# Two attention and expert layers on one core: setup taken apart into calls among the first batches, loads reordered, the order of calls written out

## The reference

```
x = x + xattn(_layernorm(x), ctx, bias (4,16,512,77), mask, L0 weights)      # softmax over 77
x = x + ffn(_layernorm(x), w_router, wi, wo)     # top 2 of 8 experts, capacity 64, gelu, 128->512->128
x = x + xattn(_layernorm(x), ctx, attn_mask (512,77) with padding, L1 weights)
x = x + ffn(_layernorm(x), gate_w, gate_b, expert_w, expert_b)   # top 2 of 8 true + 2 null experts
```

## Time and profile before

| | |
|---|---|
| median of three runs | 414.07 us |
| the profiled execution | 414.41 us, span 412.6 us |
| TensorE matmul busy | 335.0 us (81%), 3625 instructions |
| VectorE busy | 267.6 us (65%) |
| GpSimd busy | 188.9 us (46%) |
| ScalarE busy | 172.1 us (42%) |
| HBM read | 17.53 MB |

### The profile page before, as it was taken

One profiled execution on the slowest core, in us unless ns is written; L12 is line 12 of the kernel. 1 busy time (PEld: TensorE's weight loads), 2 busy tenths in 40 slices (PEclk: granted clock), 3 DMA queues, 4 the chain that ended last, 5 costly groups with the idle time before them and its releaser, 6 DMA issues.

```text
span 412.6 us, 8817 instructions
## 1 busy us (share of the span) xinstructions
PE 335.0 (81%) x3625; PEld 250.1 (61%) x3633; DVE 267.6 (65%) x629; ACT 172.1 (42%) x317; POOL 188.9 (46%) x211
## 2 busy tenths in 40 slices
PE   3985597587899999999999989999776886787382
PEld 2982366265679777788778867886634553454120
DVE  0132558849666855766766766775898889877632
ACT  3000323132736546374646636563623443353222
POOL 9202534364737334646536443520763376254214
PEclk9999996959999999999999999999995999699867
DMA  3996314130504022000000000000000000000000
GB/s 98 251 366 207 93 39 132 32 101 0 132 2 132 4 54 79 0 3 2 0 3 1 3 2 2 2 2 0 4 1 25 2 2 1 27 2 0 27 1 25
DMA packets 26363, 19.15 MB, mean 46 GB/s; under 512 B 1909, under 2 KB 24275, under 8 KB 26323
## 3 DMA queue, kind: packets, MB, share of 16 engines
q1 hardware_dynamic: 26163, 18.56, 15.4%
q0 software_dynamic: 160, 0.02, 0.3%
HBM read 17.53 MB, written 1.05 MB: 45 GB/s over the span
## 4 chain that ended last, share of the span: by engine, by line
PE 60%; DVE 21%; ACT 9%; issue 4%; POOL 3%; SPq 1%; DMA 1%; POOLq 0%; DVEq 0%; ACTq 0%
PE PB L809 10%; PE HBK L891 8%; PE EBK L906 7%; DVE SC L1228 7%; PE SP L790 6%; ACT PT L533 5%; PE SP L771 4%; PE HBK L914 4%; DVE mx L1230 3%; DVE rc L1236 3%; PE HBK L956 2%; PE SP L775 2%; PE MB L748 2%; PE EBK L956 2%; PE PB L815 1%
## 5 line engine op out<-in xcount | busy, mean ns | idle before, releaser
L351 POOL TENSOR_TENSOR SC<-SC,mx 128x1232 f32<-128x1232 f32 x32 | 72.0, 2250 | 136.9 <-DVE mx L1230 136.8
L533 ACT COPY PT<-SP 128x512 f32<-128x512 f32 (+1 forms) x96 | 44.4, 521 | 41.0 <-PE SP L790 41.0
L790 PE MATMUL SP<-ident,SC 128*128 128x128 f32 x320 | 48.1, 298 | 12.3 <-ACT SC L525 6.4
L790 PEld LDWEIGHTS SP<-ident,SC 128*128 128x128 f32 x320 | 40.4, 154 | 21.8 <-issue 12.5
L525 ACT ACTIVATE SC<-SC 128x1232 f32<-128x1232 f32 x32 | 39.3, 1229 | 33.5 <-POOL SC L351 33.4
L1230 DVE TENSOR_REDUCE mx<-SC 128x16 f32<-128x1232 f32 x32 | 46.0, 1436 | 1.1
L1236 DVE RECIPROCAL rc<-PB 128x128 f32<-128x128 f32 x32 | 30.5, 952 | 16.5 <-PE PB L809 16.5
L809 PE MATMUL PB<-PT,VB 128*32 128x128 f32 x768 | 30.8, 299 | 12.5 <-ACT PT L533 11.7
L891 PE MATMUL HBK<-ein,wi_s 128*128 128x128 f32 x256 | 36.8, 287 | 2.6 <-ACT hT L551 2.6
L891 PEld LDWEIGHTS HBK<-ein,wi_s 128*128 128x128 f32 x256 | 31.0, 191 | 10.9 <-ACT hT L551 5.5
L551 ACT ACTIVATE hT<-HBK 128x512 f32<-128x512 f32 x32 | 19.1, 597 | 41.1 <-PE HBK L891 41.0
(11 more groups left out here) (174 smaller groups left out, 577.1 us busy)
## 6 DMA issues: line engine op xcount, KB each, us to landing
BI<-in_fside_Bx16xSxS SPq DMA_DIRECT2D x8, 1232.0 KB, 6.3
wi_s<-in_L_ffn_wi SPq DMA_DIRECT2D x1, 2048.0 KB, 10.8
X<-in_x SPq DMA_DIRECT2D x4, 256.0 KB, 3.6
out<-acc SPq DMA_DIRECT2D x4, 256.0 KB, 2.1
MI<-in_mask_BxSxS_ik SPq DMA_DIRECT2D x8, 77.0 KB, 7.0
ew_s<-in_L_ffn_expert_w SPq DMA_DIRECT2D x1, 512.0 KB, 4.9
ctxn<-in_ctx SPq DMA_DIRECT2D x1, 154.0 KB
am<-in_fside_SxS SPq DMA_DIRECT2D x1, 154.0 KB, 2.5
```

The costliest lines, as they stand in the source:

```text
L351: g.tensor_tensor(S4, S4, m4, ALU.subtract).then_inc(s["shifted"], 1)
L533: sc.copy(PT[:, c0:c1, :].rearrange("p c t -> p (c t)"), SP[:, n, 0:(c1 - c0) * P]).then_inc(s["PTs"], 1)
L790: last = te.transpose(SP[:, n, (c - c0) * P:(c - c0 + 1) * P], SC[i % 2][:, c * P:(c + 1) * P], ident[:])
```

## The change

The setup's steps become functions that are called among the calls of the first two batches, most constants are filled by VectorE instead of GpSimd (`fill`), the loads have semaphores by group and a new order, and `stretch` is gone: each engine's program is a list of calls (309 on TensorE, 197 on VectorE, 219 on ScalarE, 119 on GpSimd, from 296, 188, 212 and 112). The arithmetic is the same. Values of batch 0 go to PB and EBK, of the others to HBK and EBK; keys of layer 1 to EBK. Some calls have further waits (`gelu` on `m_eo`, `f_xTcopy` on `m_logits`, `a_xTr` on the routing), since the order no longer implies them. The gate bias and expert bias loads move from GpSimd's queue to SP's.

```diff
@@ sync
-            for n in range(4):
-                sp.dma_start(W[:, n, :], w0[n]).then_inc(s["ld_w"], 16)
...
-            load_bias(0)
...
+            load_x(0, "ld_x0")
             sp.dma_start(ctxn[:], ctx_in.rearrange("b j d -> j b d")).then_inc(s["ld_ctx"], 16)
+            load_w(0, 1, "ld_wa")
+            load_w(0, 0, "ld_wa")
+            load_col(0, 1, "ld_ca")
+            load_col(0, 0, "ld_ca")
+            load_mask(0, 0)
+            load_bias(0, 0)
...
+            load_mask(0, 1)
+            load_bias(0, 1)
...
+            load_mask(1, 0)
+            load_bias(1, 0)
+            load_mask(1, 1)
+            load_bias(1, 1)
+            sp.dma_start(wo_s[:], wo.rearrange("e (c f) d -> f e c d", c=FC)).then_inc(s["ld_moe"], 16)
...
@@ scalar
+                if f > 0 or e >= 4:
+                    act.wait_ge(s["m_eo"], NE // 2 * f + (e - 4) // 2 + 1)
...
@@ tensor
-            stretch(0, 0, None, None, None, None)
-            stretch(1, 0, 0, 0, None, None)
-            for a in range(2, B):
-                stretch(a, 0, a - 1, 0, a - 2, 0)
...
+            turn_ctx()
+            turn_weights((0, 1), "ld_wa", 0)
+            a_xTr(0)
+            keys(0)
+            query(0, 0)
+            attn_scores(0, 0, 0)
+            turn_weights((2, 3, 6), "ld_wb", 1)
+            values(0)
+            attn_scores(0, 1, 0)
+            turn(0, 0, 0)
+            turn_weights((4, 5, 7), "ld_wc", 3)
+            turn(0, 0, 1)
+            value_bias(0)
+            attn_scores(0, 2, 0)
+            keys(1)
+            weigh_values(0, 0)
+            value_bias(1)
+            turn(0, 1, 0)
+            values(1)
...
@@ vector
+            def fill():
+                for t, x in ((half[:], -0.5), (identb[:], 0.0), (rowmask[:], 1.0), (incl[:], 1.0), (strict[:], 1.0),
...
+                    v.memset(t, x).then_inc(s["c_dset"], 1)
...
+            fill()
+            a_stats(0, 0)
+            a_norm(0, 0)
+            copy_first()
+            scale_q(0, 0)
+            softmax_max(0, 0, 0)
+            spread_bv()
+            softmax_max(0, 1, 0)
+            add_bias(0)
+            mask_values(0)
...
```

More of the change, by code:

```diff
@@ L489, in _ @@
[L489 to L492 removed]
+            identity()
+            identity_bf16()
+            head_rows()
+            a_rstd(0)
+            block_rows()
+            mask_out(0, 0)
+            block_keys(0, 0, "k_kb")
+            block_keys(1, 0, "k_kb")
+            shift(0, 0)
+            mask_out(0, 1)
+            shift(0, 1)
@@ L677, in _ @@
[L677 to L686 removed]
+            copy_ctx(0, 1)
@@ new lines, in _ @@
+            attn_scores(1, 1, 0)
+            project(0, 3, 0)
+            turn(1, 0, 0)
+            values(3)
+            f_xTr(0)
+            turn(1, 0, 1)
+            logits0(0)
+            attn_scores(1, 2, 0)
+            weigh_values(1, 0)
+            turn(1, 1, 0)
+            positions(0)
+            project(1, 0, 0)
+            turn(1, 1, 1)
+            attn_scores(1, 3, 0)
+            dispatch(0, 0)
+            weigh_values(1, 1)
+            turn(1, 2, 0)
+            turn(1, 2, 1)
@@ new lines, in _ @@
+            positions(2)
+            up(1, 7)
+            turn(3, 1, 0)
+            down(1, 3)
+            turn(3, 1, 1)
+            combine(1, 0)
+            project(3, 0, 0)
+            combine(1, 1)
+            weigh_values(3, 1)
+            attn_scores(3, 3, 0)
+            dispatch(2, 0)
+            a_xTr(4)
+            turn(3, 2, 0)
+            project(3, 1, 0)
+            turn_C(2, 0)
+            turn(3, 2, 1)
+            dispatch(2, 1)
+            weigh_values(3, 2)
+            turn_C(2, 1)
@@ new lines, in _ @@
+            turn_C(2, 2)
+            turn(3, 3, 0)
+            turn_C(2, 3)
+            turn(3, 3, 1)
+            project(3, 2, 0)
+            up(2, 0)
+            query(4, 1)
+            weigh_values(3, 3)
+            up(2, 1)
+            attn_scores(4, 0, 1)
+            up(2, 2)
+            project(3, 3, 0)
+            up(2, 3)
+            attn_scores(4, 1, 1)
+            up(2, 4)
+            down(2, 0)
+            up(2, 5)
+            f_xTr(3)
+            down(2, 1)
+            up(2, 6)
@@ new lines, in _ @@
+            logits0(3)
+            turn(4, 0, 0)
+            turn(4, 0, 1)
+            down(2, 2)
+            attn_scores(4, 2, 1)
+            weigh_values(4, 0)
+            positions(3)
+            up(2, 7)
+            turn(4, 1, 0)
+            turn(4, 1, 1)
+            down(2, 3)
+            attn_scores(4, 3, 1)
+            combine(2, 0)
+            project(4, 0, 1)
+            combine(2, 1)
+            weigh_values(4, 1)
+            dispatch(3, 0)
+            turn(4, 2, 0)
+            turn(4, 2, 1)
```

1582 lines of the change are left out of this document (953 added, 629 removed).

## The result

The changed kernel took **381.23 us** (median of four runs, 378.92 to 382.82) beside 413.99 for the kernel before (413.46 to 415.3): a ratio of 0.920, with a 95% interval of 0.915 to 0.925. The forecast was 383.8 with a range of 369 to 396. The profiled execution took 381.17 us with a span of 379.5. The same kernel went again with the experiments: 383.4 us (378.11 to 390.28, ratio 0.928, 0.921 to 0.935). Medians and ranges here count every execution, while a ratio compares only those within 1.5% of the fastest of their kernel, so a median and its ratio need not agree.

A forecast was written before the change was run, and what follows sets the result against it. It took setup alone to hold the first 30.8 us, the attention chain to pace the opening and TensorE the middle. Terms −25.8 + 1.2 − 3 − 1 − 2 = −30.6 from 414.4 gave 383.8 us, range 369 to 396.

The forecast's parts named there:

- Term A: Start of batch 0: with X loaded first, first scores at 13.0 us instead of 38.8, −25.8 us.
- The −24.4: Start of batch 0: the start's gain if batch 0's normalising waits for GpSimd's rowmask selects, 0.35 us each.
- Term B: First scores to first up-projection: setup matmuls moved in are nearly free, +76.3 us instead of +75.1, so +1.2 us.
- I keep the low level until about 30: Opening: assumes TensorE's clock stays at its low level, 1.2 GHz, until about 30 us.
- The first L720 at the low level: Opening: a sign the forecast is right, the first of the setup's value matmuls running at the low clock level.
- Term C: Middle, 113.9 to 300 us: the new call order takes 3 of 10.6 us idle, −3, between 0 and −8.
- Terms D and E: 300 to 380 us, VectorE's list almost unchanged: −1; the end, last tile's scores and expert matmuls reordered: −2.
- middle stretches under 45: Middle: a sign that the order gains more than counted, batches under 45 us apart instead of 45.5 to 46.5.
- Setup only moves: Opening: batch 0 waits for each setup call, +12 us from first scores to first up-projection, 395 us; chance 0.12.
- loads hold the first tiles: Start: the bias or the weights behind it arrive 4 us late, 388 us; chance 0.05.
- the order wins more: Whole kernel: gaps at batch edges close, middle and end give more, an early clock rise included, 368 us; chance 0.20.
- The slow rival: Opening: the clock stays low, +32 us there, 422 us in all; sign L771 at 1.41 beyond 40 us; chance 0.02.

The follow-up runs named there:

- Experiment 3: The changed kernel with batch 0's load of X issued behind the first bias instead of first: 392.13 us, ratio 0.954.
- experiment 2: The changed kernel's loads and batch order, but all setup calls ahead of batch 0 on every engine again: 417.8 us, ratio 1.021.
- experiment 4: The kernel before, with its two key matmuls of 308 columns run three times over ahead of the values: 409.94 us, ratio 0.998.
- experiment 6: The changed kernel with nine added matmuls at the start, batch 3's values moved earlier and 40 filler matmuls in TensorE's holes at 48 to 61 us: 377.84 us.
- e1_old_rest: The changed kernel up to the first up-projection, then every engine's calls in the order of before: 388.62 us, ratio 0.931.

## Why the prediction was right or wrong

- **Term A, right.** Forecast −25.8, measured −26.9. First scores at 11.95, inside 13 ± 1.5. X landed in 2.8 us and not in 3.6, which is most of the difference. Experiment 3 shows that this chain sets the whole program, one for one, experiment 2 that the new loads without the interleaving don't shorten it, at least in that version. The lock between the normalising and the rowmask selects didn't come: the selects ran at 6.21 beside the normalising at 6.28, which took 1.27 us (1.21 before). The −24.4, which I had worked out by the rule of the Trainium skill ("SBUF — State Buffer", Who interferes with whom), is not borne out for this pair.
- **Term B, the step that failed** is "I keep the low level until about 30". In the profiled execution the clock was up before the first scores, and B was −2.6 in place of +1.2. In the repeat the level was low until about 30, and B was +0.7. So the term was sized about rightly for the clock it assumed: the fourth tile's scores, forecast at +26.5, came at +24.8 in the repeat (36.92), at +18.1 in the first execution; batch 1's first scores, forecast at +36.5, at +36.8 (48.92) and +30.0. The rule of the Trainium skill ("TensorE: Matmul & The Clock Gate", Part 1) that I set aside, with 380 by it, was right in the execution that took 381.17. The repeat did the same work at the start and stayed low until about 30, so the rule as I used it doesn't tell the two apart. What I held against it, the setup's run at the low level, was no lasting property, as experiment 4 shows. "The first L720 at the low level" was wrong in one execution, right in the other.
- **Behind the first four tiles** the lead shrank. In the first execution batch 1's first scores came at +30.0, 6.5 us ahead of the forecast; the first up-projection, forecast at +76.3, came at +72.5, 3.8 ahead. Tile (1,2)'s scores were at +51.1. What I hadn't placed is the wait of 4.27 us for VectorE ahead of 50.78 and the low level behind it, until past 63.09. That this low level is what shrank the lead fits experiment 6, where B is 69.15 us without it. I had written that the old gap of 4.26 us would be smaller. It is the same one, come 32 us sooner.
- **Term C, right**: −2.9 against −3, and +3.3 when the old order is put back at the same clock. By their queries (83.31 to 268.32, four distances) batches stand 46.25 us apart on average, as forecast (45.5 to 46.5); singly they stand 42.1 to 49.3 apart, and 44.7 to 49.4 in the kernel before, so "middle stretches under 45" was no usable sign.
- **Terms D and E**, −3 together, measured −0.8 in one execution and +4.8 in the other. By granted clocks of 0.87 and 0.84 the level was low for 2 × (0.13 × 39.6 + 0.16 × 71.6) = 33 us of the last 111; by 0.83 and 0.78 for 2 × (0.17 × 40.8 + 0.22 × 76.0) = 47 of 117. The first execution is the fair pair: the kernel before had 0.87 and 0.85 there, nearly its clocks, and −0.8 is what was gained. So I had sized D and E too high by some 2 us, as far as one pair of traces tells. D and E of `e1_old_rest`, at lower clocks than the first, can't settle it.
- **The rivals.** "Setup only moves" asked for +12 in B and is ruled out; "loads hold the first tiles" too: TensorE's only wait for a DMA in the whole trace is the first, for ctxn, VectorE's only one is for X, and the values at 14.43 waited 0.72 for ScalarE. Half of "the order wins more" came true: an early clock, without the larger C, D and E. The slow rival's sign, L771 (now L996) at 1.41 beyond 40 us, did come in the first execution, at 63.09, and yet that one was fast: the low stretch ended by 71.24, where scores take 0.80 again. It marked the clock falling a second time and not the rival, which would have needed 31 us more in B.
- **The range.** The bounds of the five terms, added plainly, give −53 to −11, which is 361 to 403 us. The prediction says 371 to 395 and doesn't say how; both results lie inside either.

How the gain divides between order and clock is not settled. A and C fell by 29.6 to 29.8 us in both executions; the rest moved with the clock, from −3.4 to +5.6. Two comparisons of spans, one execution each, both give 24: a late rise in both (412.6 − 388.6 = 24.0), and an early one in both (26.8 − 2.7 = 24.1). But the repeat lost 4.8 us in D and E at lower clocks than the kernel before had, so the first would be some 29 at like clocks there. From 24 to 29 of the 33 us between the profiled spans are then the order's, as an estimate from these spans, and the rest the clock's.

**Open:** why the same code finds the upper level at 11 us once and at 30 another time; why the clocks of D and E differ between executions of the same code; and how the interleaving fares with the old loads.

## What to carry to other kernels

Setup that batch 0 doesn't need belongs among the first batches, placed call by call, when the profile shows a chain whose every microsecond arrives at the end: test that by delaying its first load. Price a forecast at both clock levels for stretches that border on one, and read the level from durations of like instructions. Before moving a call that something waits for, ask what stood behind it on its engine; and measure one filler before filling a hole with many.

## What the runs showed that I had not expected

- One kernel had two openings. Up to the first scores its two traces differ by 0.2 us; the clock then came up at 11 us in one and at 30 in the other, and the spans were 379.5 and 388.6.
- The page's clock reads 9 tenths ahead of the first rise though the instructions run at the low level (L932 at 2.37 us in the repeat, 1.30 in the other execution).
- TensorE's 18 us of value matmuls, without a gap, left the level low in the profiled execution of the kernel before; behind 5.14 us of key matmuls they ran at the upper level for 10 us (L723, 1.28). One trace each, so which of the two the setup does by itself isn't known.
- X took 2.8 us as the first DMA and 6.9 us as the eighth.
- A normalising on VectorE and four selects on GpSimd ran side by side and hardly grew (1.27 us against 1.21, and 1.26 against 1.25 in `e2_setup_first`, where the selects ran alone), while the kernel before had such a normalising stretched to 3.20 beside a subtraction of two operands.
